# Cross-attention in fp32: Wo and V cross DRAM in fp32 and are split into parts on arrival; the row maximum moves to the end of its slot

## The chip, the cores and the metric

The kernel runs on one core of a Trainium2 chip. The core has five engines that run their own instruction queues and meet at semaphores: TensorE (PE, matrix products), VectorE (DVE), ScalarE (ACT), GpSimd (POOL) and SyncE (SP), which here issues nearly all DMAs. The metric is the time of one execution on the device, in microseconds.

## The reference

```python
a = layer_norm(ctx, gamma, beta)                  # ctx: 8 x 64 x 1024
Q = (x @ Wq.T)                                    # x: 8 x 1024 x 1024, 16 heads of 64
K, V = a @ Wk.T, a @ Wv.T
scores = Q K^T / 8  per head;  masked keys -> -inf
attn = softmax(scores over the 64 keys)
out = x + tanh(gate) * ((attn @ V) @ Wo.T)
```

Everything is fp32 and the output is 8192 x 1024.

## The kernel before

**Products in three parts.** Each fp32 operand is split into a high part, its rounding to fp32r, and a low part, the rest. `three` (lines 1192 to 1196) multiplies low x high, high x low and high x high. ScalarE makes the high parts by a rounding copy, VectorE (or GpSimd) the low parts by a subtraction.

**Stages.** First K, V and M are made: M holds Wq's product with K per batch, so that scores = x times M. PE works through 48 weight blocks in `TURNS`. M's blocks are copied from PSUM into the ring `m_stage` and stored to `m_scratch`, or straight into `b_raw`. V comes out in two column halves: ScalarE writes the scaled high part (`copy_v_hi`, line 718) and VectorE the low part (`split_v_lo`, 967), both into `v_out`; SyncE stores each half (`store_v`, 424).

**The main loop** has 224 steps in 32 rounds of 7. Rounds 0 to 15 make the scores of 512 rows each, rounds 16 to 31 the output. A round is one Strassen level: seven products P1, P5, P6, P3, P7, P2, P4, each a step of two groups of 12 matmuls (`item`, 1274). A step's left operand lies in `a_ring`: ScalarE writes its high part (`split_a_hi`, 738), VectorE the low part (`split_a_lo`, 974), one step ahead. The right operands of all seven products lie in `parts`, 16 KiB per partition each. In the score rounds they are refilled every 14 steps from M (`split_b_hi`, `split_b_lo`, `sum_b`; the steps are in `REFILL`). VectorE adds each product into `c_out` (`add_out`, 1058), and later products of the same round wait for these adds (1291 to 1302). An engine's order inside a step is written out in its loop: for VectorE lines 1136 to 1175. A step has two slots, z = 2s and 2s + 1.

**Softmax.** From step 98 on, units of 128 columns of scores run through slots fixed by `SOFT`: SyncE loads a unit (`load_s`, 455), which for a later unit waits until the one seven before it has been transposed; VectorE takes the row maximum (`row_max`), ScalarE the exponentials, VectorE the sums, GpSimd scales. The first 16 units are transposed by PE (`transpose_p`), rounded by ScalarE (`split_p_hi`) and their low part is made by VectorE (`split_p_lo`); PE transposes the next unit only when the last low part is there. Later units are turned by VectorE (`turn_blocks`), stored and fetched again by SyncE (`store_p`, `fetch_p`) and their low parts made by GpSimd. `values` (1265) multiplies by V, which lies in `v_diag` as two 64-wide diagonal blocks per head pair, in both parts, loaded per batch by `load_v` (489).

**Wo.** Wo's seven operands are three quarters of Wo and four sums of them. In steps 2 to 90 SyncE loads eighths of Wo (`load_wo_quarter`), VectorE makes the sums (`sum_wo`), ScalarE and VectorE split all seven pieces of each eighth (`round_wo`, `split_wo_lo`; 56 pieces, at the steps that `wo_step` gives) and ScalarE's queue stores them to `wo_split_scratch`. From step 106 on, SyncE loads both parts of the seven operands into `parts` in 28 DMAs (`load_wo_part`, 525; called at 608 to 610). Output rounds start with step 112.

Of the kernel before, what the change touches and what calls it, by code (L numbers as in the profile page):

```python
# [19 lines left out]
def xattn_kernel(nc, x, x_t, ctx_x, mask, wq_b, wk_t, wv_t, wo_t, gamma, beta, gate, out):  # L20
# [24 lines left out]
    v_scr = nc.dram_tensor("v_scratch", [B * S, NC, 2, P], F32, kind="Internal").ap()  # L45
    wo_scr = nc.dram_tensor("wo_split_scratch", [7, P, 2, HC, HD], F32, kind="Internal").ap()
# [3 lines left out]
    with ExitStack() as ctx:  # L50
# [35 lines left out]
        wo_sum = at("wo_sum", 208, [P, 4, QW])  # L86
        wo_ring = at("wo_ring", 212, [P, 3, 2, QW], F32R)
# [4 lines left out]
        v_out = [at("v_out0", 32, [P, CT, HC, 2, P], F32R), at("v_out1", 96, [P, CT, HC, 2, P], F32R)]  # L92
# [56 lines left out]
        wo_split_stored = sems("wo_split_stored", 3)  # L149
# [6 lines left out]
        v_hi_made = sem("v_hi_made")  # L156
        v_lo_made = sem("v_lo_made")
# [19 lines left out]
        v_in = sems("v_in", 2)  # L177
        s_in = sems("s_in", PROBS)
# [124 lines left out]
        WO_ORDER = (P1, P5, P7, P6, P3, P2, P4)  # L303
        WO_PIECES = 7 * 8

        def wo_step(w):
            return 14 * ((w + 6) // 9) + (0, 1, 3, 4, 4, 5, 6, 6, 7)[(w + 6) % 9]

        def wo_pieces(s):
            return [w for w in range(WO_PIECES) if wo_step(w) == s]  # L310

        def wo_quads(w):
            return [wo_quarter[:, w // 7 % 2, i, :] for i in range(4)]

        def wo_sums_by(w):

            return 4 * (w // 7) + (0, 1, 2, 3, 3, 3, 4)[w % 7]

        def wo_source(w):
            k = WO_ORDER[w % 7]  # L320
            if k in (P1, P3, P2):
                return wo_quads(w)[{P1: 0, P3: 3, P2: 2}[k]]
            return wo_sum[:, (P5, P7, P6, P4).index(k), :]
# [31 lines left out]
        def soft_slot(u):  # L355
            return SOFT[u]

# [24 lines left out]
        def _(sp):  # L382
# [4 lines left out]
            def load_wo_quarter(i):  # L387
# [3 lines left out]
                if i >= 2:  # L391
                    sp.wait_ge(wo_lo_made, 7 * (i - 1))
# [31 lines left out]
            def store_v(half):  # L424
                sp.wait_ge(v_lo_made, CT * (half + 1))
                to = v_scr[:, HC * half:HC * (half + 1)].rearrange("(i p) g t e -> p i (g t e)", p=P)
                sp.dma_start(to, v_out[half][:].rearrange("p i g t e -> p i (g t e)").bitcast(F32)
                             ).then_inc(v_stored[half], 16)
# [26 lines left out]
            def load_s(u):  # L455
                base, j = u // 8 * HT, u % 8
                if u == 0:
                    for i in range(3):
                        sp.wait_ge(wo_split_stored[i], 16 * ((WO_PIECES + 2 - i) // 3))
# [29 lines left out]
            def load_v(b, four):  # L489
                for h in range(2):  # L490
                    rr = slice(h * HEAD, (h + 1) * HEAD)
                    src = v_scr[b * S:(b + 1) * S, 4 * four:4 * four + 4, :, rr].rearrange("s g t e -> s (g t) e")
                    to = v_diag[rr, 4 * four:4 * four + 4, :, rr].rearrange("s g t e -> s (g t) e")
                    sp.dma_start(to.bitcast(F32), src).then_inc(v_in[four], 16)
# [30 lines left out]
            def load_wo_part(k, c):  # L525
                if c == 0:
                    sp.wait_ge(item_done, 2 * (14 * (B - 1) + 7 + k + 1))
                if k == 0 and c == 0:
                    for i in range(3):
# [155 lines left out]
        def _(act):  # L685
# [155 lines left out]
            for t in range(ITEMS):  # L841
# [10 lines left out]
                elif c == NC - 1 and half == 0:  # L852
                    for i in range(CT):
                        copy_v_hi(0, i)
# [511 lines left out]
```

## Time and profile before

| | us |
|---|---|
| median of 3 runs | 1492.25 (1492.04 to 1496.14) |
| the profiled execution | 1494.74 |
| its span, first to last instruction | 1493.0 |
| PE busy / VectorE / ScalarE / GpSimd | 1467.3 / 1163.7 / 894.1 / 537.7 |
| bytes read from and written to HBM | 198.26 MB, 145.75 MB |

The profile is of one execution. Times are us from the first instruction. Matmuls are pipelined: one of 512 columns is shown with about 390 ns, and the next starts some 0.23 us after it. "Idle" is the time for which an engine had nothing running before an instruction, put down to what ended it.

### The profile page before, as it was taken

The page shows a single profiled execution, that of the slowest core. Times are in us where ns is not written, and L with a number is a line of the kernel's source. Part 1 is how long each engine was busy: PE and PEld are TensorE (multiplying, and loading weights), DVE is VectorE, ACT ScalarE, POOL GpSimd, SP SyncE. Part 2 cuts the span into 40 slices and gives each one's busy share as a digit, 9 for nine tenths or more (in the row PEclk, how much of TensorE's full clock was granted, in tenths as well). Part 3 has the DMA queues.
Part 4 walks back from the last instruction along what each step waited for, and adds up shares of the span by engine and source line. Part 5 has one row for each costly group of instructions (what it writes and reads, how often), then busy time and mean ns, then how long its engine had stood idle before and what let it go on. Part 6 is the DMA issues. An engine that isn't in the chain of part 4 may idle for free.

```text
span 1493.0 us, 20136 instructions
## 1 busy us (share of the span) xinstructions
PE 1467.3 (98%) x6624; PEld 1194.6 (80%) x6624; DVE 1163.7 (78%) x1349; ACT 894.1 (60%) x1894; POOL 537.7 (36%) x364
## 2 busy tenths in 40 slices
PE   6999999999999999999999999999999999999999
PEld 5666788888888888888787788888888888888887
DVE  6445788787878787979866788888888888888843
ACT  4556655455555555555776667766777776677521
POOL 5334000000000000000124566677766667776640
PEclk9999999999999999999999999999999999999999
DMA  7699865657575747474579988788887878888732
GB/s 281 215 376 391 292 216 198 216 199 231 183 233 174 242 159 257 142 253 132 168 254 328 297 250 243 235 248 244 265 267 238 234 242 248 242 265 266 212 118 84
DMA packets 303144, 348.51 MB, mean 233 GB/s; under 512 B 35648, under 2 KB 177088, under 8 KB 303040
## 3 DMA queue, kind: packets, MB, share of 16 engines
q1 hardware_dynamic: 287808, 332.54, 70.2%
q10 hardware_dynamic: 15232, 14.68, 2.8%
q8 instruction: 53, 0.87, 0.2%
q14 instruction: 51, 0.42, 0.1%
HBM read 198.26 MB, written 145.75 MB: 230 GB/s over the span
## 4 chain that ended last, share of the span: by engine, by line
PE 89%; DVE 3%; DMA 3%; issue 1%; SPq 1%; ACT 1%; POOL 1%; DVEq 0%; ACTq 0%; POOLq 0%
PE banks L1194 29%; PE banks L1196 29%; PE banks L1195 29%; PE banks L1223 3%; DMA m_scratch<-m_stage 1%; DMA probs<-s_scratch 1%; DVE parts L983 1%; DMA b_raw<-m_stage 1%; DVE a_ring L977 1%; PE banks L1262 0%; SPq L475 0%; DVE b_raw L1003 0%; DMA b_raw<-m_scratch 0%; PE banks L1188 0%; DVE a_sum L1047 0%
## 5 line engine op out<-in xcount | busy, mean ns | idle before, releaser
L1194 PE MATMUL banks<-parts,a_ring 128*128 128x512 f32 x1792 | 699.5, 390 | 4.3 <-DVE a_ring L977 3.5
L1196 PE MATMUL banks<-parts,a_ring 128*128 128x512 f32 x1792 | 697.5, 389 | 0.0
L1195 PE MATMUL banks<-parts,a_ring 128*128 128x512 f32 x1792 | 697.2, 389 | 0.0
L1194 PEld LDWEIGHTS banks<-parts,a_ring 128*128 128x128 f32 x1792 | 336.4, 188 | 76.2 <-DVE a_ring L977 6.1
L1196 PEld LDWEIGHTS banks<-parts,a_ring 128*128 128x128 f32 x1792 | 336.3, 188 | 70.2
L1195 PEld LDWEIGHTS banks<-parts,a_ring 128*128 128x128 f32 x1792 | 336.4, 188 | 69.3
L977 DVE TENSOR_TENSOR a_ring<-a_sum,a_ring 128x1024 fp32r<-128x1024 f32 x128 | 227.1, 1774 | 76.6 <-ACT a_ring L748 76.5
L748 ACT CAST a_ring<-a_sum 128x1024 fp32r<-128x1024 f32 x128 | 134.3, 1049 | 233.8 <-PE banks L1196 205.3
L1072 DVE TENSOR_TENSOR c_out<-banks,c_out 128x1024 f32<-128x1024 f32 x158 | 192.0, 1215 | 100.4 <-PE banks L1196 98.6
L818 ACT ACTIVATE probs<-probs,neg_max 128x64 f32<-128x64 f32 x1024 | 258.6, 337 | 1.2 <-DVE neg_max L1086 1.2
L657 POOL TENSOR_TENSOR probs<-probs,row_rec 128x512 f32<-128x512 f32 x128 | 134.6, 1052 | 241.3 <-DVE row_rec L1095 241.3
L748 ACT CAST a_ring<-xq 128x1024 fp32r<-128x1024 f32 x96 | 100.8, 1050 | 168.9 <-PE banks L1196 162.4
L674 POOL MEMSET v_diag<- 128x2048 f32 x1 | 1.8, 1811 | 551.0 <-DVE parts L983 551.0
L663 POOL TENSOR_TENSOR p_parts<-p_by_key,p_parts 128x512 fp32r<-128x512 f32 x112 | 172.5, 1541 | 25.8 <-ACT p_parts L827 24.2
L977 DVE TENSOR_TENSOR a_ring<-xq,a_ring 128x1024 fp32r<-128x1024 f32 x96 | 118.0, 1229 | 35.3 <-ACT a_ring L748 35.3
L983 DVE TENSOR_TENSOR parts<-b_raw,parts 128x1024 fp32r<-128x1024 f32 x112 | 135.7, 1221 | 6.8 <-ACT parts L775 6.8
L839 ACT COPY xq<-banks 128x512 f32<-128x512 f32 x128 | 74.7, 584 | 81.2 <-PE banks L1196 75.7
L775 ACT CAST parts<-b_raw 128x1024 fp32r<-128x1024 f32 x112 | 114.3, 1048 | 2.7 <-DVE b_raw L1003 1.4
L1086 DVE TENSOR_REDUCE neg_max<-probs 128x8 f32<-128x512 f32 x128 | 85.0, 665 | 17.0 <-ACT probs L818 9.2
L634 POOL TENSOR_TENSOR w_ring<-w_raw,w_ring 128x512 fp32r<-128x512 f32 x48 | 64.8, 1372 | 77.6 <-ACT w_ring L690 77.6
L1003 DVE TENSOR_TENSOR b_raw<-b_raw 128x1024 f32<-128x1024 f32 x64 | 78.1, 1224 | 10.5 <-DMA b_raw<-m_stage 5.5
L964 DVE COPY m_stage<-banks 128x512 f32<-128x512 f32 x64 | 43.7, 690 | 53.6 <-PE banks L1223 47.1
(77 smaller groups left out, 1350.8 us busy)
## 6 DMA issues: line engine op xcount, KB each, us to landing
xq<-x_t SPq DMA_DIRECT2D x32, 1024.0 KB, 6.2
s_scratch<-c_out SPq DMA_DIRECT2D x64, 512.0 KB, 3.1
probs<-s_scratch SPq DMA_DIRECT2D x128, 256.0 KB, 4.2
c_out<-x SPq DMA_DIRECT2D x63, 512.0 KB, 5.5
out<-c_out SPq DMA_DIRECT2D x63, 512.0 KB, 4.2
b_raw<-m_scratch SPq DMA_DIRECT2D x29, 1024.0 KB, 6.8
m_scratch<-m_stage SPq DMA_DIRECT2D x16, 1792.0 KB, 14.0
p_scratch<-p_turned SPq DMA_DIRECT2D x448, 64.0 KB, 2.6
```

The costliest lines, as they stand in the source:

```text
L657: nc.gpsimd.tensor_tensor(pr, pr, rec, ALU.mult).then_inc(probs_done, 1)
L663: nc.gpsimd.tensor_tensor(p_parts[:, u % 2, 1, :], by_key(u), p_parts[:, u % 2, 0, :].bitcast(F32), ALU.subtract).then_inc(p_lo_made, 1)
L748: nc.scalar.copy(a_ring[:, s % 2, 0], a_source(n, k)).then_inc(a_hi_made, 1)
L775: nc.scalar.copy(parts[:, k, 0, c:c + 2, :], b_raw[:, B_HOME[k], c:c + 2, :]).then_inc(b_hi_made, 1)
L818: last = nc.scalar.activation(prob(u)[:, cols], prob(u)[:, cols], ACT.Exp, bias=neg_max[:, u % 2, g:g + 1])
L977: nc.vector.tensor_tensor(a_ring[:, s % 2, 1], a_source(n, k), a_ring[:, s % 2, 0].bitcast(F32), ALU.subtract).then_inc(a_lo_made, 1)
L983: nc.vector.tensor_tensor(parts[:, k, 1, c:c + 2, :], b_raw[:, B_HOME[k], c:c + 2, :], parts[:, k, 0, c:c + 2, :].bitcast(F32), ALU.subtra ...
L1072: nc.vector.tensor_tensor(c_out[:, q], bank_pair(n, k), to_add, ALU.add).then_inc(added, 1)
L1086: nc.vector.tensor_reduce(neg_max[:, u % 2, :], prob(u).rearrange("p (g s) -> p g s", s=S), AX.X, ALU.max, negate=True).then_inc(max_done, 1)
L1194: pe.matmul(to, wl, mh, start=first, stop=False, skip_group_check=joined)
L1195: pe.matmul(to, wh, ml, start=False, stop=False, skip_group_check=joined)
L1196: return pe.matmul(to, wh, mh, start=False, stop=last, skip_group_check=joined)
```

## The change

Wo: SyncE still loads the eighths, and VectorE makes the four sums, now at four steps in a row from 7 + 11i for eighth i; ScalarE's queue stores them unsplit (8 stores). Nothing is split before step 109. SyncE loads each operand whole in fp32, the three quarters from Wo itself and the four sums from the scratch, into the place of its low part. In steps 109, 110, 111, 113, 114, 115 and 116 ScalarE writes the high part in two halves, one per slot, and VectorE subtracts in place.

V: ScalarE alone writes V out, in fp32. The store and the loads carry one part. Each load lands in the place of the low part in `v_diag`; ScalarE and VectorE split it (two instructions each, on 64 partitions) three slots before its first product.

VectorE's order in a slot was sum, maximum, low part of probabilities, turn. It is now sum, low part, turn, maximum, V's low part, Wo's low part.

```diff
-    v_scr = nc.dram_tensor("v_scratch", [B * S, NC, 2, P], F32, kind="Internal").ap()
-    wo_scr = nc.dram_tensor("wo_split_scratch", [7, P, 2, HC, HD], F32, kind="Internal").ap()
+    v_scr = nc.dram_tensor("v_scratch", [B * S, D], F32, kind="Internal").ap()
+    wo_scr = nc.dram_tensor("wo_sum_scratch", [4, P, HC, HD], F32, kind="Internal").ap()
...
+        v_raw = at("v_raw", 120, [P, NC, 2, P])
+        wo_raw = [at(f"wo_raw{k}", 16 * k + 8, [P, HC, HD]) for k in range(7)]
...
+        LAST = 14 * (B - 1) + 7
+        WO_LOAD = {LAST + k + (1 if k < P2 else 2): k for k in range(7)}
+        WO_SPLIT = {LAST + k + (4 if k < P3 else 5): k for k in range(7)}
+        def wo_sum_step(i):
+            return 7 + 11 * i
...
+        def v_split(z):
+            return [(b, four) for b in range(B) for four in range(2) if values_at(16 * b + 4 * four) // 4 - 3 == z]
...
+            def load_wo_part(k):
+                sp.wait_ge(item_done, 2 * (LAST + k + 1))
...
+                sp.dma_start(wo_raw[k][:], src).then_inc(wo_part_in[k], 16)
...
-            def copy_v_hi(half, i):
+            def copy_v(half, i):
...
+            def split_wo_hi(k, h):
+                act.wait_ge(wo_part_in[k], 16)
+                part = slice(2 * h, 2 * h + 2)
+                nc.scalar.copy(parts[:, k, 0, part, :], wo_raw[k][:, part, :]).then_inc(wo_hi_made, 1)
...
+            def split_v_hi(b, four):
+                act.wait_ge(v_in[four], 32 * (b + 1))
+                for h in range(2):
+                    rr = slice(h * HEAD, (h + 1) * HEAD)
+                    nc.scalar.copy(v_diag[rr, 4 * four:4 * four + 4, 0, rr], v_raw[rr, 4 * four:4 * four + 4, 1, rr]
+                                   ).then_inc(v_hi_made, 1)
...
                     for u in units(soft_slot, z - EXP):
                         exponential(u)
+                    for b, four in v_split(z):
+                        split_v_hi(b, four)
+                    if s in WO_SPLIT:
+                        split_wo_hi(WO_SPLIT[s], z % 2)
...
+                for i in range(WO_QUARTERS):
+                    if 0 <= s - wo_sum_step(i) < 4:
+                        sum_wo(i, s - wo_sum_step(i))
                 for z in (2 * s, 2 * s + 1):
                     for u in units(soft_slot, z - SUM):
                         sum_rows(u)
-                    for u in units(soft_slot, z - MAX):
-                        row_max(u)
                     for u in units(split_slot, z):
                         if u < ON_PE:
                             split_p_lo(u)
                     for u in units(soft_slot, z - TURN):
                         if u >= ON_PE:
                             turn_blocks(u)
+                    for u in units(soft_slot, z - MAX):
+                        row_max(u)
+                    for b, four in v_split(z):
+                        split_v_lo(b, four)
+                    if s in WO_SPLIT:
+                        split_wo_lo(WO_SPLIT[s], z % 2)
...
-                        pe.wait_ge(wo_part_in[k], 64)
+                        pe.wait_ge(wo_lo_made, 2 * k + 2)
```

`split_v_lo` and `split_wo_lo` are the same with a subtraction. The waits for `v_lo_made` in the first stage become waits for `v_made`, and `values` waits for the new `v_lo_made` at the first unit of each load.

## Rows read from the trace of the kernel before

**Rows 1.** The page: busy us and share of each engine; the chain's shares.

```profile
PE 1467.3 (98%) x6624; PEld 1194.6 (80%) x6624; DVE 1163.7 (78%) x1349; ACT 894.1 (60%) x1894; POOL 537.7 (36%) x364
...
PE banks L1194 29%; PE banks L1196 29%; PE banks L1195 29%; PE banks L1223 3%; DMA m_scratch<-m_stage 1%; DMA probs<-s_scratch 1%; DVE parts L983 1%; DMA b_raw<-m_stage 1%; DVE a_ring L977 1%; PE banks L1262 0%; SPq L475 0%; DVE b_raw L1003 0%; DMA b_raw<-m_scratch 0%; PE banks L1188 0%; DVE a_sum L1047 0%
```

**Rows 2.** Busy times by stretch: its length, each engine (instructions), clock, DMA share, GB/s.

```profile
165.00:200.00 35.00, 33.84 (x145) 27.09 (x146) 33.13 (x32) 20.44 (x23) 0.00 (x0) 1.00 0.70 244
200.00:700.00 500.00, 500.00 (x2207) 414.01 (x2206) 414.10 (x418) 263.65 (x306) 0.00 (x0) 1.00 0.59 199
...
769.94:827.03 57.09, 53.87 (x253) 44.09 (x251) 39.80 (x60) 39.07 (x114) 21.87 (x15) 1.00 0.94 301
...
860.00:1480.00 620.00, 620.00 (x2737) 513.35 (x2737) 507.87 (x610) 408.13 (x1115) 413.45 (x266) 1.00 0.78 232
```

The five busy times are those of PE, its weight loads, VectorE, ScalarE and GpSimd.

**Rows 3.** Waits of PE: waited for, us in total, times, longest.

```profile
PE banks L1262 <- DVE p_parts L1108: 3.9, 3, 1.8
PE banks L1194 <- DVE a_ring L977: 3.5, 3, 1.4
...
PE banks L1194 <- POOL p_parts L663: 1.1, 1, 1.1
```

**Rows 4.** Timeline of VectorE and PE at the hand-over: start, us, what, idle before.

```profile
161.89 2.36 DVE L1003 TENSOR_TENSOR b_raw<-b_raw 128x1024 f32<-128x1024 f32 x2 [5.53 <-DMA b_raw<-m_stage]
164.16 1.22 DVE L977 TENSOR_TENSOR a_ring<-xq,a_ring 128x1024 fp32r<-128x1024 f32 x1
...
168.71 1.40 DVE L969 SCALAR_TENSOR_TENSOR v_out<-banks,v_scale,v_out 128x512 fp32r<-128x512 f32 x2
...
165.44 0.50 PE L1194 MATMUL banks<-parts,a_ring 128*128 128x512 f32 x1 [1.37 <-DVE a_ring L977]
```

**Rows 5.** DMA by stretch: its length, clock, share, GB/s.

```profile
134.00:161.00 27.00, 1.00 1.04 404
```

**Rows 6.** DMA issues: count, KB each, median us to landing.

```profile
parts<-wo_split_scratch SPq DMA_DIRECT2D x28, 512.0 KB, 7.7
...
v_scratch<-v_out SPq DMA_DIRECT2D x2, 2048.0 KB, 11.9
```

**Rows 7.** Groups by line: count, busy us, mean ns of one, idle before.

```profile
L983 DVE TENSOR_TENSOR parts<-b_raw,parts 128x1024 fp32r<-128x1024 f32 x112 | 135.7, 1221 | 6.8 <-ACT parts L775 6.8
...
L775 ACT CAST parts<-b_raw 128x1024 fp32r<-128x1024 f32 x112 | 114.3, 1048 | 2.7 <-DVE b_raw L1003 1.4 <-DMA b_raw<-m_scratch 0.8 <-issue 0.4
...
L1025 DVE TENSOR_TENSOR wo_ring<-wo_sum,wo_ring 128x256 fp32r<-128x256 f32 x32 | 13.0, 418 | 0.0
L782 ACT CAST wo_ring<-wo_sum 128x256 fp32r<-128x256 f32 x32 | 12.5, 403 | 2.6 <-DVE wo_sum L1021 1.5 <-issue 1.1
```

**Rows 8.** Timeline at step 55: VectorE's add, and PE's first product of P4.

```profile
464.78 1.22 DVE L1072 TENSOR_TENSOR c_out<-banks,c_out 128x1024 f32<-128x1024 f32 x1
...
466.37 0.39 PE L1194 MATMUL banks<-parts,a_ring 128*128 128x512 f32 x1
```

**Rows 9.** Timeline at the softmax start: late row maxima, and PE's waits for low parts.

```profile
800.12 0.69 DVE L1086 TENSOR_REDUCE neg_max<-probs 128x8 f32<-128x512 f32 x1 [2.38 <-DMA probs<-s_scratch]
...
805.21 0.63 PE L1262 MATMUL banks<-ident,probs 128*128 128x128 f32 x4 [1.41 <-DVE p_parts L1108]
...
817.62 0.69 DVE L1086 TENSOR_REDUCE neg_max<-probs 128x8 f32<-128x512 f32 x1 [1.94 <-DMA probs<-s_scratch]
...
819.05 0.63 PE L1262 MATMUL banks<-ident,probs 128*128 128x128 f32 x4 [1.81 <-DVE p_parts L1108]
```

**Rows 10.** Timeline at step 120: a GpSimd sum and VectorE's low part beside it.

```profile
852.07 2.38 POOL L651 TENSOR_TENSOR a_sum<-xq,a_sum 128x1024 f32<-128x1024 f32 x1
...
852.25 3.28 DVE L977 TENSOR_TENSOR a_ring<-a_sum,a_ring 128x1024 fp32r<-128x1024 f32 x1
```

**Rows 11.** Timeline of SyncE's queue: issues before the first store of turned probabilities.

```profile
814.07 2.96 SPq L531 DMA_DIRECT2D parts<-wo_split_scratch  x3
817.07 1.69 SPq L475 DMA_DIRECT2D p_scratch<-p_turned  x1
```

More of the change, by code:

```diff
@@ L298, in refills, with wo_quads @@
             return [(rnd, q) for rnd in range(B) for q in range(14) if refill_step(rnd, q) == s]
[L303 to L323, printed above, removed]
+        WO_QUAD = {P1: 0, P3: 3, P2: 2}
+        WO_SUMS = (P5, P7, P6, P4)
+        WO_QUARTERS = 2 * HC
+        LAST = 14 * (B - 1) + 7
[3 more added lines that the diff above has]
+            return 7 + 11 * i
+        def wo_quads(i):
+            return [wo_quarter[:, i % 2, quad, :] for quad in range(4)]
         def quad_rows(ap, n, q):
@@ L457, in load_s @@
                 if u == 0:
-                    for i in range(3):
-                        sp.wait_ge(wo_split_stored[i], 16 * ((WO_PIECES + 2 - i) // 3))
+                    for i in range(2):
+                        sp.wait_ge(wo_sum_stored[i], 16 * (WO_QUARTERS // 2))
                 elif u >= PROBS + ON_PE:
@@ L523, in after_product @@
                     store_quad(n, 2)
[L525 to L529, printed above, removed]
-                        sp.wait_ge(wo_split_stored[i], 16 * ((WO_PIECES + 2 - i) // 3))
-                sp.dma_start(parts[:, k, :, c, :].bitcast(F32), wo_scr[k, :, :, c, :]).then_inc(wo_part_in[k], 16)
+            def load_wo_part(k):
+                sp.wait_ge(item_done, 2 * (LAST + k + 1))
+                if k in WO_QUAD:
+                    r, c = divmod(WO_QUAD[k], 2)
+                    src = wo_t[r * HD:(r + 1) * HD, c * HD:(c + 1) * HD].rearrange("(c p) n -> p c n", p=P)
+                else:
+                    for i in range(2):
+                        sp.wait_ge(wo_sum_stored[i], 16 * (WO_QUARTERS // 2))
+                    src = wo_scr[WO_SUMS.index(k)]
+                sp.dma_start(wo_raw[k][:], src).then_inc(wo_part_in[k], 16)
             def slot(z):
@@ L548, in slot @@
                         load_x(y + 1)
-                    for i in range(8):
-                        if s == (2 + i if i < 2 else wo_step(7 * (i - 1) - 1) + 1):
+                    for i in range(WO_QUARTERS):
+                        if s == (2 + i if i < 2 else wo_sum_step(i - 2) + 5):
                             load_wo_quarter(i)
@@ L607, in _ @@
                 slot(z)
-                for i in range(28):
-                    if 2 * (14 * (B - 1) + 8) + (18 * i // 28) == z:
-                        load_wo_part(i // 4, i % 4)
+                if z % 2 == 0 and z // 2 in WO_LOAD:
+                    load_wo_part(WO_LOAD[z // 2])
             for g in range(2):
@@ L862, in _ @@
             for i in range(CT):
[L863 removed]
+                copy_v(1, i)
             for s in range(STEPS):
@@ L866, in _ @@
                     split_a_hi(s + 1)
-                for w in wo_pieces(s - 1):
-                    store_wo_split(w)
+                for i in range(WO_QUARTERS):
+                    if s == wo_sum_step(i) + 5:
+                        store_wo_sums(i)
                 if s > 0:
@@ L1104, in turn_blocks, with split_v_lo @@
                                     prob(u).rearrange("p (t h k) -> p h t k", h=4, t=4)).then_inc(turned, 1)
+            def split_v_lo(b, four):
+                dve.wait_ge(v_hi_made, 4 * b + 2 * four + 2)
+                for h in range(2):
+                    rr = slice(h * HEAD, (h + 1) * HEAD)
+                    hi, lo = (v_diag[rr, 4 * four:4 * four + 4, t, rr] for t in range(2))
+                    nc.vector.tensor_tensor(lo, v_raw[rr, 4 * four:4 * four + 4, 1, rr], hi.bitcast(F32), ALU.subtract
+                                            ).then_inc(v_lo_made, 1)
             def split_p_lo(u):
@@ L1121, in _ @@
                     split_k_lo(half)
-                elif c == NC - 1 and half == 0:
-                    for i in range(CT):
-                        split_v_lo(0, i)
             for q in range(2, 4):
@@ L1133, in _ @@
             sum_a(0, P5)
-            for i in range(2):
-                split_v_lo(1, i)
             for s in range(STEPS):
@@ L1141, in _ @@
                     split_a_lo(s + 1)
-                if s == 0:
-                    for i in range(2, CT):
-                        split_v_lo(1, i)
                 if n < ROUNDS:
```

97 lines of the change are left out of this document (38 added, 59 removed).

## The prediction

> **What bounds the kernel now.** I read the busy shares and the chain's shares first [rows 1]. TensorE (PE) is busy for 98% of the span, and its three product lines make 87% of the chain that ended last. VectorE is busy for 78% and ScalarE for 60%, so trimming either is worth only what PE waits for. Next I read PE by stretches [rows 2]. From 200 to 700 us and from 860 to 1480 us PE is busy for every microsecond, at 500.00 / 2207 = 0.2266 us a product, so a step of 24 products takes 5.44 us. The granted clock is 1.00 in every stretch, the 2.4 GHz level. In these 1120 us an edit can only lose time, unless it removes products, and this one removes none. PE idles 1.16 us in 165 to 200 and 57.09 - 53.87 = 3.2 us in 769.94 to 827.03. The waits of PE [rows 3] name who ends them: 3.9 us in three waits for VectorE's low part of the probabilities, 3.5 us in three waits for a_ring's low part, 1.1 us for GpSimd's low part. These 8.5 us, and some restart behind each, are nearly all that the change can give back. So three places count: the hand-over to the main loop, the start of the softmax with the new Wo work in it, and VectorE's slack in the dense stretches.
>
> **V out in fp32, and half of its store.** The four low halves of V's first column half fall where PE is dense: nothing. Those of the second stand in front of the first main steps. VectorE starts at 161.89 on b_raw, is busy from then on, and ends a_ring's first low part at 164.16 + 1.22 = 165.38; PE starts at 165.44 and has idled 1.37 [rows 4]. Two V instructions (1.40) lie before the second a_ring low part, two more behind it. Without them that part waits for ScalarE's high part instead (1.05, nearest row L775 [rows 7]), which needs the a_sum that VectorE makes just before: step 1 gains only about 0.1, but steps 2 to 5, which run off the same backlog, are freed: about 1.0 with restarts. What starts the backlog is the DMA of b_raw out of m_stage. The DMA engines are full from 134 to 161 us (share 1.04, 404 GB/s) [rows 5], and the first V store, of 2048 KB [rows 6], is issued in that stretch. It becomes 1024 KB: 1.05 MB / 404 GB/s = 2.6 us of a full queue. If all of it reaches b_raw, VectorE starts at 159.3, the first wait (1.37 and a restart of 0.1) goes, and PE's last V tile, which ends 1.37 before 165.44, is late next. Bounds: -3.1 (all that PE loses there) to -1.1 (queue unmoved). I take -2.8, since the queue is full right across.
>
> **The Wo sums in steps 7 to 88.** Removed: 56 high parts (ScalarE, 0.40), 56 low parts (VectorE, 0.42), 56 stores. Kept: the 32 sums, of the low parts' shape, at 0.42 [rows 7]. PE is dense there, so the removal is worth nothing. But the sums move, to four steps in a row from 7 + 11i. For i = 0 and 4 they fall on steps 7 to 10 and 51 to 54, where VectorE refills the seven B operands almost without a pause, and where the old order has next to no Wo work. There the add that P4 waits for ends at 464.78 + 1.22 = 466.00 and P4 starts at 466.37 [rows 8]: 0.37 of slack. Three sums at 0.42 (less when back to back) put about 1.0 ahead of it; I let pauses eat 0.2. So 0.8 - 0.37 + 0.1 = 0.5, twice, and i = 5 (two sums there) just about none: +1.0. Bounds: 0 (the sums fill pauses) to +1.5.
>
> **V split in the loop.** 16 loads are split by 32 ScalarE and 32 VectorE instructions of 256 elements; nearest rows 0.40 and 0.42 [rows 7], bounds 0.25 to 0.6 each. Each split is 0.8 on each engine, last in its slot, three slots before its products. The first stands ahead of a low part of the probabilities on which PE already waits; the row maximum now goes behind that part (0.6 saved), so +0.2 net. Of the 15 others those in the dense stretch meet VectorE at 507.87 / 620 = 82% [rows 2]: hidden, 0. Were their cover gone, the seven that end an odd slot would cost some 0.3 each, +2.
>
> **Wo's operands split between steps 109 and 116.** Added in 57 us: 14 high parts at 1.05 (ScalarE, nearest row L775) and 14 low parts at 1.22 (VectorE, L983) [rows 7]. Busy times were 39.07 and 39.80 of 57.09 [rows 2]. Now they are 39.07 + 14.7 = 53.8 and 39.80 + 17.1 = 56.9: both are full, VectorE wholly. The 28 part loads of 512 KB become 7 of 1024 KB (14.7 MB to 7.3 MB) [rows 6], where the DMA share was 0.94 [rows 2]; they lead their use by three steps and are on no path. What was on the path is in [rows 9]. VectorE idled 2.38 and 1.94 us for a row maximum whose scores were late, and only then did the low part for which PE waited (1.41 at 805, 1.81 at 819). The new order puts that part in front of the maximum. That removes the second wait and, with quicker scores, the first: -3.5 with restarts. Against it stand the halves. I followed both engines from step 109, each serving its queue in order. ScalarE falls about 1 us behind per step, so that the high part of unit 13 ends near 808 in place of 804; the low part before PE's transposes of unit 14 comes 1.3 us late, that before unit 15 some 2.1, an earlier one 0.3: 3.8 with restarts. In addition VectorE and GpSimd block each other. A GpSimd sum from 852.07 to 854.45 makes a_ring's low part, begun at 852.25, last 3.28: it ends 1.08 after the sum does [rows 10], where it takes 1.22 alone [rows 4]. GpSimd is busy 21.87 of 57.09 [rows 2], mostly just behind a VectorE instruction of one input; I count one of its long sums on the path, at about half of 2.38: +1.2. So 3.8 + 1.2 - 3.5 = +1.5. Bounds: -3.5 (all hidden) to +7 (VectorE's 56.9, five or six halves blocked for 1 us, and some 2 us in which it must idle for ScalarE). The Trainium skill has the exclusion as a rule (SBUF — State Buffer, Who interferes with whom): a VectorE instruction with two SBUF inputs and a GpSimd instruction that reads SBUF never run together, and whichever starts first blocks the other. By that rule the trace agrees, at 3.28; and all 14 new low parts are of that sort, which speaks for the dear end of the range.
>
> **Steps 117 to 122.** PE waits for GpSimd's part near 845 (1.1) [rows 3] and for the a_ring part of [rows 10] (1.4). Their chain comes from SyncE, which stores the first turned probabilities late: it issues three Wo part loads in 2.96 us just before [rows 11]. Without those it fetches them some 2.7 us earlier, and ScalarE, which heads its queue with that wait, follows. I take half of 2.5 + restarts: -1.4; bounds -2.9 to +1 (the last halves of step 116 in front of it).
>
> **Sum.** -2.8 + 1.0 + 0.2 + 1.5 - 1.4 = -1.5. The profiled execution took 1494.74 (span 1493.0 and 1.74 around it), 2.49 above the median shown. It would take 1493.2, and the median 1490.7.
>
> **Rivals.** (a) The softmax start clears: the halves fit into pauses, of which each engine has 17 to 18 us. All three places give back: -3.1 + 0.5 + 0.2 - 3.5 - 2.9 = -8.8, 1483.5. For it: those pauses and the lighter DMA. Against: 56.9 of 57.1 us. (b) Slower: the halves fill VectorE from step 109 to 118, and a_ring's low parts come behind them. A step of 24 + 3 products takes at least 6.1 us there, and the two a_ring parts 2.3 of them, so they lead PE by some 4 us; it decides once the backlog passes that. Price +7 there, nothing back in 117 to 122, V's odd splits +1: -2.8 + 1.0 + 0.2 + 7 + 1 = +6.4, 1498.7. For it: the ledger and [rows 10]. Against: steps 112 and 117 have no halves and let it catch up. (c) The change does what it says and the relief doesn't reach PE: the V store isn't what b_raw waits for, and the waits at 805 and 819 are only replaced: -1.1 + 1.0 + 0.2 + 0.3 = +0.4, 1492.7.
>
> **How the numbers follow.** Forecast 0.40, (a) 0.27, (b) 0.22, (c) 0.11. What can be told from no change is 0.3%, 4.5 us: faster is below 1487.8, slower above 1496.7. The forecast's own range is 1487 to 1494. Faster: (a) and a tail of the forecast, 0.30; slower: (b), 0.22; same 0.48. Range 1484.5 to 1497.5: it leaves out the far halves of (a) and (b).
>
> **What would show it.** Step 0 starts at or just after 164.0 us: the V store's part is right; at 165.4 it is not. PE waits of about 0.4 for an add at P4 in steps 13 and 55: the sums. From step 109 to 116, VectorE above 95% busy and PE waits for its p_parts that add up to 4 to 5 us: the halves. None of these waits, and (a) holds; waits for a_ring too, and (b) does. A first fetch of turned probabilities before 826 us: SyncE's relief. I am wrong if PE has gaps in 860 to 1480, or if its gaps between 165 and 860 add up to under 4 or over 16 us.

## The result and the profile after

The changed kernel takes 1517.39 us (median of 4 runs, 1517.17 to 1519.59). The kernel before took 1493.65 beside it (4 runs, 1492.04 to 1496.14). The ratio is 1.0161, with a 95% interval of 1.0141 to 1.018: 24 us slower, where 1.5 faster was forecast. The profiled execution took 1517.17, its span 1515.4.

The page after, shares of busy time, then those waits of PE that lie in the main loop (waited for, us in total, times, longest); they answer to [rows 1] and [rows 3]:

```profile
PE 1476.1 (97%) x6624; PEld 1200.3 (79%) x6624; DVE 1176.2 (78%) x1331; ACT 901.1 (59%) x1884; POOL 537.4 (35%) x364
...
PE banks L1195 <- DVE a_ring L976: 15.3, 9, 2.1
...
PE banks L1263 <- DVE p_parts L1115: 7.0, 3, 3.0
...
PE banks L1195 <- DVE c_out L1071: 0.7, 2, 0.4
```

The busy shares hardly moved. What moved are the waits: a_ring's low part from 3.5 us in three waits to 15.3 in nine, the low part of the probabilities from 3.9 to 7.0. GpSimd's 1.1 has gone. (These are idle times as the profile has them, counted from the modelled end of the last product. In the text behind, a gap or a wait of PE is counted from when the next product was due, 0.227 us behind the start of the last one, which gives 0.16 more: the gaps of 2.24 below are the 2.08 of the profile.) The same stretches as in [rows 2], and the length of one half-clock episode (length, busy time of PE, PEld, DVE, ACT, POOL with instructions, granted clock, DMA share, GB/s):

```profile
165.00:200.00 35.00, 35.00 (x156) 29.00 (x155) 29.95 (x27) 20.10 (x22) 0.00 (x0) 1.00 0.68 233
200.00:700.00 500.00, 499.26 (x2201) 412.48 (x2200) 394.54 (x364) 244.59 (x251) 0.00 (x0) 1.00 0.52 176
769.94:827.03 57.09, 51.74 (x224) 41.93 (x223) 52.89 (x64) 45.20 (x113) 23.84 (x14) 0.91 0.56 183
...
860.00:1480.00 620.00, 606.95 (x2656) 500.38 (x2657) 514.10 (x631) 416.86 (x1145) 411.90 (x267) 0.99 0.77 229
...
1040.70:1044.10 3.40, 3.40 (x10) 2.67 (x9) 3.40 (x4) 1.29 (x6) 3.25 (x2) 0.51 0.32 77
```

The first stretch is now dense. The last, full before, has lost 13 us of PE and some clock. The sharpest reading comes from the start of each step's first product on PE, after minus before, in us: -3.4 at step 7; -1.7 at step 70; -0.7 from 104 to 112; +3.5 at 113; +6.5 at 119; +4.9 at 120; +5.0 from 121 to 134; then +7.2 at 135 and up at each of 149, 163, 177, 191 and 205; +22.4 at 206 and to the end. So about 17.5 of the 22.4 us come from six places 14 steps apart.

This is the first of them, between 940 and 950 us: VectorE, ScalarE and GpSimd in turn (start, us, engine, line, form; idle before and what ended it).

```profile
940.89 0.65 DVE L1085 TENSOR_REDUCE neg_max<-probs 128x8 f32<-128x512 f32 x1
943.72 3.82 DVE L1110 TENSOR_TENSOR v_diag<-v_raw,v_diag 64x256 fp32r<-64x256 f32 x2 [2.19 <-ACT v_diag L829]
947.58 1.23 DVE L1071 TENSOR_TENSOR c_out<-banks,c_out 128x1024 f32<-128x1024 f32 x1
948.72 1.22 DVE L976 TENSOR_TENSOR a_ring<-a_sum,a_ring 128x1024 fp32r<-128x1024 f32 x1
...
940.95 2.02 ACT L814 ACTIVATE probs<-probs,neg_max 128x64 f32<-128x64 f32 x8
942.87 0.82 ACT L829 CAST v_diag<-v_raw 64x256 fp32r<-64x256 f32 x2
...
943.42 2.40 POOL L649 TENSOR_TENSOR a_sum<-xq,a_sum 128x1024 f32<-128x1024 f32 x1
945.78 1.48 POOL L661 TENSOR_TENSOR p_parts<-p_by_key,p_parts 128x512 fp32r<-128x512 f32 x1
```

Read it in this order. VectorE is free at 941.5, and its next instruction is V's low half. That needs ScalarE's high half, which is queued behind eight exponentials and ends at 943.69: 2.19 of idling. In that pause GpSimd started a sum, at 943.42, which holds VectorE's first low half up to its end at 945.82 (2.38 in place of 0.42); GpSimd's next instruction then holds the second (1.41). The two halves take 3.82 in place of 0.84. The add and a_ring's low part, for which PE waits, were queued behind. Step 135 starts at 949.99, 2.24 late. The add starts 6.0 us after step 134 does (941.62). Before, at the same place, it started 0.2 us after it (936.65), and a_ring's low part, itself slowed by a GpSimd sum, ended at 941.93, 0.84 ahead of step 135 (942.77):

```profile
936.85 1.23 DVE L1072 TENSOR_TENSOR c_out<-banks,c_out 128x1024 f32<-128x1024 f32 x1 [0.27 <-PE banks L1196]
938.97 2.96 DVE L977 TENSOR_TENSOR a_ring<-a_sum,a_ring 128x1024 fp32r<-128x1024 f32 x1 [0.89 <-ACT a_ring L748]
```

So a block by GpSimd and some idling lay in this stretch before as well: 1.74 of block on a_ring's part (2.96 - 1.22) and 1.16 of idling (0.27 + 0.89). The 2.19 and the 3.82 took the place of these and brought about 3.1 us more; 0.84 of it went into the margin and 2.24 reached PE.

Behind two of the six gaps the products then come every 0.43 us in place of 0.227 for 3.4 us. PE after the gap before step 191:

```profile
1309.25 0.50 PE L1195 MATMUL banks<-parts,a_ring 128*128 128x512 f32 x1 [2.08 <-DVE a_ring L976]
...
1309.83 0.39 PE L1197 MATMUL banks<-parts,a_ring 128*128 128x512 f32 x1
1310.05 0.45 PE L1195 MATMUL banks<-parts,a_ring 128*128 128x512 f32 x1
1310.30 0.63 PE L1196 MATMUL banks<-parts,a_ring 128*128 128x512 f32 x1
1310.73 0.63 PE L1197 MATMUL banks<-parts,a_ring 128*128 128x512 f32 x1
```

The granted clock is 0.51 over such an episode (the last row of stretches), the 1.2 GHz level; each costs half its length, 1.7 us. Six gaps of 2.24 are 13.4, two episodes 3.4, and restarts (the second product behind such a gap starts 0.34 us after the first in place of 0.227) make the rest of 17.5. Between steps 112 and 118 lie two more, of 3.4 us behind a wait of 2.55 (791.1 to 793.7) and of 6.8 us, 815.3 to 822.1, around the end of one of 3.12 (813.1 to 816.2).

The new groups of instructions by line (busy, mean ns, idle before and its releaser):

```profile
L1110 DVE TENSOR_TENSOR v_diag<-v_raw,v_diag 64x256 fp32r<-64x256 f32 x32 | 33.4, 1043 | 21.3 <-ACT v_diag L829 20.8
L1024 DVE TENSOR_TENSOR parts<-wo_raw,parts 128x1024 fp32r<-128x1024 f32 x14 | 18.3, 1304 | 0.9 <-ACT parts L784 0.9
L784 ACT CAST parts<-wo_raw 128x1024 fp32r<-128x1024 f32 x14 | 14.6, 1045 | 0.0
L829 ACT CAST v_diag<-v_raw 64x256 fp32r<-64x256 f32 x32 | 12.8, 399 | 0.4
```

ScalarE's halves last what the nearest rows said (0.40 and 1.05). VectorE's V halves have a median of 0.42 but a mean of 1.04, and in front of them it idles for ScalarE for 20.8 us. That line alone holds the reason.

### The profile page after: what moved, and what is told of

The parts are those of the page before. It is cut to its first block, busy times and chain, and to the rows that moved or that the text cites. A ratio compares the mean times of both kernels' runs of the same rounds, so it can differ in the third digit from the quotient of the medians.

```text
span 1515.4 us, 19964 instructions
## 1 busy us (share of the span) xinstructions
PE 1476.1 (97%) x6624; PEld 1200.3 (79%) x6624; DVE 1176.2 (78%) x1331; ACT 901.1 (59%) x1884; POOL 537.4 (35%) x364
## 4 chain that ended last, share of the span: by engine, by line
PE 84%; DVE 7%; ACT 3%; issue 3%; DMA 1%; SPq 1%; POOL 0%; DVEq 0%; ACTq 0%
PE banks L1195 27%; PE banks L1196 27%; PE banks L1197 27%; PE banks L1224 3%; DVE a_ring L976 2%; ACT probs L814 2%; DVE c_out L1071 1%; DVE parts L982 1%; DMA m_scratch<-m_stage 1%; DVE b_raw L1002 1%; ACT xq L842 0%; PE banks L1263 0%; ACT v_diag L829 0%; DVE row_sum L1090 0%; PE banks L1189 0%
## 5 line engine op out<-in xcount | busy, mean ns | idle before, releaser
L1195 PE MATMUL banks<-parts,a_ring 128*128 128x512 f32 x1792 | 702.8, 392 | 16.0 <-DVE a_ring L976 15.3
L976 DVE TENSOR_TENSOR a_ring<-a_sum,a_ring 128x1024 fp32r<-128x1024 f32 x128 | 215.8, 1686 | 81.0 <-ACT a_ring L746 81.0
L661 POOL TENSOR_TENSOR p_parts<-p_by_key,p_parts 128x512 fp32r<-128x512 f32 x112 | 169.3, 1512 | 26.6 <-ACT p_parts L823 25.7
L1090 DVE TENSOR_REDUCE row_sum<-probs 128x8 f32<-128x512 f32 x128 | 85.5, 668 | 0.0
```

The source lines that it names most:

```text
L661: nc.gpsimd.tensor_tensor(p_parts[:, u % 2, 1, :], by_key(u), p_parts[:, u % 2, 0, :].bitcast(F32), ALU.subtract).then_inc(p_lo_made, 1)
L976: nc.vector.tensor_tensor(a_ring[:, s % 2, 1], a_source(n, k), a_ring[:, s % 2, 0].bitcast(F32), ALU.subtract).then_inc(a_lo_made, 1)
L1090: nc.vector.reduce_sum(row_sum[:, u % 2, :], prob(u).rearrange("p (g s) -> p g s", s=S), AX.X).then_inc(sum_done, 1)
L1195: pe.matmul(to, wl, mh, start=first, stop=False, skip_group_check=joined)
```

## The experiments

"Step n" below is the start of its first product against that of the kernel before (runs' profiles). A profile's start of the main loop differs from another's by itself: in the six kernels with the old way of V, step 7 lies between -1.0 and +0.9, mean -0.05. Times are medians; the kernel before took 1493.5 to 1494.3 beside them.

**e1 and e2: place, or time?** e1 moves the V splits that ended an odd slot one slot on:

```diff
- ... if values_at(16 * b + 4 * four) // 4 - 3 == z]
+ ... if (values_at(16 * b + 4 * four) // 4 - 2) // 2 * 2 == z]
```

> The changed kernel with one edit: the V splits that sit at the end of an odd slot (7 of them in the dense stretch) move to the even slot behind it, so that VectorE makes a_ring's low part first. Theory (place): each of the 2.24 us gaps of PE in steps 121 to 205 comes from V's low halves standing before the add and a_ring's low part while they wait for ScalarE and then for GpSimd's sum. Then no gap over 0.3 us is left after 865 us and the clock stays at 1.00 there: 17.5 us less than 1517.4, about 1500. Rival (amount): VectorE lacks the time for 0.8 us more wherever it is put: gaps go to other steps, 1512 to 1518.

e2 moves ScalarE's high halves alone, one slot ahead of VectorE's low halves:

```diff
-                    for b, four in v_split(z):
+                    for b, four in v_split(z + 1):
                         split_v_hi(b, four)
```

> The changed kernel with ScalarE's high half of each V split one slot earlier; VectorE's low halves stay where they are. It tells the wait for ScalarE from the block by GpSimd. If only the wait for ScalarE (behind 2 us of exponentials) costs: the gaps go, 1500. If only GpSimd's sum blocks: they stay at 2.24 us, 1517. Theory (both in turn): VectorE starts the halves some 2 us earlier, ahead of the sum, may be blocked once by a shorter GpSimd instruction: gaps under 1 us, 1501 to 1507.

e1: 1504.06, ratio 1.0072 [1.0056, 1.0089]. The gaps of 2.24 are gone, and 0.50 at each following step, with some new waits around step 121, came in their place: 4 us more than expected, so the place was most of the loss, not all. e2: 1500.64, ratio 1.0049 [1.0034, 1.0064], and from 861 us on PE has no gap at all: the difference stays at +5.7. Its stretch of the dense part, and the V splits' two groups:

```profile
860.00:1480.00 620.00, 618.72 (x2730) 512.32 (x2731) 521.55 (x637) 420.03 (x1149) 420.73 (x269) 1.00 0.78 230
```

```profile
L1110 DVE TENSOR_TENSOR v_diag<-v_raw,v_diag 64x256 fp32r<-64x256 f32 x32 | 26.1, 817 | 0.6
L829 ACT CAST v_diag<-v_raw 64x256 fp32r<-64x256 f32 x32 | 12.9, 404 | 0.4
```

The idle before the low half fell from 21.3 to 0.6 us with the same instructions in the same number. VectorE's work was never the trouble; it is even still blocked now and then (mean 0.82). What cost was VectorE standing for ScalarE, with everything else queued behind. Of the three readings put down for e2 this fits the one that I did not hold, that the wait for ScalarE alone costs; e12 below shows the share that the block had as long as VectorE waited.

**e3 and e4: one part alone.** e3 is the kernel before with the V part only, e4 the changed kernel with V as before.

> The kernel before with only the V part of the change. Theory: it carries the gain at the hand-over (-3.4 us at step 12) and the loss in the dense stretch (+17.5), and about +1.5 at the first low part of the probabilities: 1493.7 + 15.6 = 1509. Rival (the parts need each other: the gaps come only with the later row maximum): the hand-over alone, 1490 to 1492.

> The changed kernel with V as before (Wo part and row maximum kept). Theory: no gap after 865 us, the hand-over gain is lost: 1517.4 - 17.5 + 3.4 - 1 = 1502. Rival (Wo's part is what costs in the dense stretch too): above 1508.

e3: 1511.64, ratio 1.0122 [1.0107, 1.0137], 2.6 above what was expected. Step 7 at -3.2, step 134 at -1.7, then the six gaps (and three half-clock episodes): +17.4 at the end. e4: 1500.19, ratio 1.0047 [1.0032, 1.0062]. The gaps of 0.5 at steps 13 and 55, step 70 at +1.1, step 112 at +0.5, step 118 at +7.2, +5.3 at the end, nothing after 861 us. The parts add up: +17.4 and +5.3 against +22.4.

**e5: the row maximum last, alone.**

```diff
                     for u in units(soft_slot, z - TURN):
                         if u >= ON_PE:
                             turn_blocks(u)
+                    for u in units(soft_slot, z - MAX):
+                        row_max(u)
```

> The kernel before with the row maximum moved to the end of its slot, V and Wo as before. My blind working gave this edit the whole of the two waits at 805 and 819 us (-3.5). Theory 'the maximum was in the way': both waits go, steps 112 to 118 come out 2.5 to 3.5 us earlier, total about 1490.5 to 1491.5. Rival 'the order moves the wait': the low part goes first, but the maximum, and with it the exponentials and the later units, come as late as before; the waits change place, and the total stays within 1 us of 1494.

1492.48, ratio 0.9989 [0.998, 0.9998]. In its trace the wait at 819 is gone, that at 805 went from 1.57 to 0.81, that at 732 from 0.80 to 0.19; one of 0.90 for GpSimd's part at 831 is new. At the end -1.9 in the profile, -1.0 by the medians. In between the two theories: at most half of what I had given this edit.

**e6 and e7: Wo.** Both are the kernel before with the Wo part alone. e6 moves the sums off the refill steps; e7 leaves them and makes ScalarE's Wo halves a slot early.

```diff
-            return 7 + 11 * i
+            return 14 + 14 * (i // 2) + 4 * (i % 2)
```

```diff
-                    if s in WO_SPLIT:
-                        split_wo_hi(WO_SPLIT[s], z % 2)
+                    if (z + 1) // 2 in WO_SPLIT:
+                        split_wo_hi(WO_SPLIT[(z + 1) // 2], (z + 1) % 2)
```

> The kernel before with the Wo part alone (V and the order of the row maximum as before), and its sums moved from steps 7 + 11 i to steps 14 + 14 (i / 2) + 4 (i mod 2), which keeps them off steps 8 to 13 of every 14, where VectorE refills the B operands. Theory 'the sums stood in front of P4's add and a_ring's low part': no gap of 0.5 at steps 13 and 55 and none of 0.17 at 69, difference to the kernel before 0.0 from step 7 to 101. Rival 'the gaps come from something else of the Wo part' (its loads, its stores): they stay, or show at other steps, +1.2 in all. Steps 109 to 120 have the halves as in the changed kernel: if these alone are the cost there, +6.5 to +7.5 by step 118 and +5.5 at the end, total 1499 to 1500; if half of it came from V, +3, total 1496.5.

> The kernel before with the Wo part alone, and ScalarE's high halves of Wo one slot earlier, so that VectorE's low half finds its high half made. Theory 'as with V, VectorE stands waiting for ScalarE, whose half is queued behind the exponentials': the loss of steps 112 to 118 falls from about +7 to +2 or +3, total about 1496. Rival 'both engines have more work than time there and GpSimd's sums block VectorE': the order of the halves frees nothing, the loss stays at +6 or more, total 1500 or above.

e6: 1501.09, ratio 1.0045 [1.0031, 1.0058]. No gap from step 7 to 101: the difference is +0.85 throughout. So the sums stood in the way, as forecast. By step 118 it is +8.6, 1 more than expected. e7: 1503.45, ratio 1.0057 [1.0041, 1.0074], step 118 at +10.3, a loss of 8.7 from step 109 on against e6's 7.8: the mend that healed V made this worse. Here VectorE doesn't wait for ScalarE (0.9 us of idle in the changed kernel's row above). What it does instead, VectorE, then GpSimd, in the changed kernel from 784 us:

```profile
784.73 1.21 DVE L1024 TENSOR_TENSOR parts<-wo_raw,parts 128x1024 fp32r<-128x1024 f32 x1
785.86 3.42 DVE L976 TENSOR_TENSOR a_ring<-xq,a_ring 128x1024 fp32r<-128x1024 f32 x1
789.21 1.21 DVE L1071 TENSOR_TENSOR c_out<-banks,c_out 128x1024 f32<-128x1024 f32 x1
790.34 0.67 DVE L1085 TENSOR_REDUCE neg_max<-probs 128x8 f32<-128x512 f32 x1
790.94 1.21 DVE L1024 TENSOR_TENSOR parts<-wo_raw,parts 128x1024 fp32r<-128x1024 f32 x1
792.07 0.67 DVE L1090 TENSOR_REDUCE row_sum<-probs 128x8 f32<-128x512 f32 x1
792.77 0.20 DVE L1094 RECIPROCAL row_rec<-row_sum 128x8 f32<-128x8 f32 x1
792.89 0.64 DVE L1115 TENSOR_TENSOR p_parts<-banks,p_parts 128x512 fp32r<-128x512 f32 x1
...
784.75 3.46 POOL L649 TENSOR_TENSOR a_sum<-xq 128x1024 f32<-128x1024 f32 x1
```

VectorE has no pause from one end to the other. The Wo half (784.73) and GpSimd's sum (784.75) start together; the sum first waits out the half and lasts 3.46 in place of 2.4, then a_ring's part waits out the sum and lasts 3.42 in place of 1.22. The low part of the probabilities (792.89) is last in this queue, and PE's next transposes, at 793.68, wait 2.55 us for it. VectorE's instructions of 770 to 834 us took 7.0 us in all above the medians of their forms, against 0.6 before.

**e8, e9 and e10: V without the stall.** On the kernel before: e8 has the V part with high halves a slot early, and the first batch's two halves a slot earlier still. e9 adds the row maximum last. e10 is e9 with the first batch's halves one slot later than in the changed kernel, behind the first low part of the probabilities, and the high halves early as in e2:

```diff
- ... if values_at(16 * b + 4 * four) // 4 - 3 == z]
+ ... if values_at(16 * b + 4 * four) // 4 - 3 + (b == 0) == z]
```

> The kernel before with the V part alone, ScalarE's high halves of V one slot before VectorE's low halves, and both halves of the first batch one slot earlier still. Theory: the hand-over gain stays (-3.25 at step 7), no gap at 135, 149, 163, 177, 191 and 205 (0 in place of 2.24 each and their half clock), and the first split costs 0 to 1 us at steps 102 to 104: -2.2 to -3.2 at the end, total 1491 to 1492 against 1494, a gain of 0.15 to 0.2%. Rival 'a split costs wherever it stands, since VectorE has no slack': 0.5 or more at each of the 14 later splits, total above 1498.

> The kernel of e8 (V part alone, its halves early) with the row maximum last in its slot as well; Wo as before. Theory 'the two gains are apart, V's at the hand-over (-2.9 at step 7) and the maximum's at 732, 805 and 819 us (-1.9)': -3.5 to -4.5 at the end, total 1489.5 to 1490.5 against 1493.5. Rival 'both reach the same row of waits around 805 to 860, and what one gives the other can't give again' (both came to -1.9 at the end): -2 to -3, total about 1491.5.

> As e9, but of V's first batch both halves go one slot after the place of the changed kernel, not one before: the low half then stands behind the low part of the first probabilities. In e3 that low half in front of it made PE wait 2.44 in place of 0.80 at 731, in e8 one slot earlier 1.11, with 0.47 at step 103 besides. Theory 'it is the order around unit 0': 0 to 0.3 there and none at step 103, so 0.5 to 1.0 less than e9, total 1489 to 1490. Rival: the low half is then late for its own products at step 104 (PE waits for v_lo_made, 0.5 to 2), and nothing is gained on e9.

e8: 1492.41, ratio 0.9991 [0.9982, 0.9999]. e9: 1490.87, 0.9978 [0.9969, 0.9987]. Both lie 0.4 above their forecasts. e10: 1488.91, 0.9968 [0.9955, 0.998], the best version, 4.8 us under the kernel before. Its waits of PE in the main loop (the rest of its list lies ahead of it):

```profile
PE banks L1203 <- DVE a_ring L984: 2.4, 2, 1.6
...
PE banks L1203 <- POOL p_parts L668: 0.7, 1, 0.7
PE banks L1271 <- DVE p_parts L1123: 0.3, 1, 0.3
```

The 8.5 us of [rows 3] are down to 3.4, both as the profile counts. Around step 104 the order decided: e3, with the low half in front of the first low part of the probabilities, waits 2.44 there; e8, a slot earlier, 1.11 with 0.47 at step 103; e10 nothing. From step 104 on e10 gains 2.6 where e5 gained 1.5 and e8 lost none; the extra is at step 118, where e5 and e8 wait 0.9 for GpSimd's part (831 us) and e10 does not; why it doesn't I have not taken apart.

**e11, e12 and e13: GpSimd's sums in two.** From step 90 on each sum for a_ring is two instructions of half the size: in e11 on the Wo part alone, in e12 on e3, in e13 on e10.

```diff
-                nc.gpsimd.tensor_tensor(a_sum[:, A_SUM[k]], *sum_operands(n, k)).then_inc(sum_made, 1)
+                one, two, op = sum_operands(n, k)
+                to, c = a_sum[:, A_SUM[k]], HC // 2
+                nc.gpsimd.tensor_tensor(to[:, 0:c], one[:, 0:c], two[:, 0:c], op)
+                nc.gpsimd.tensor_tensor(to[:, c:], one[:, c:], two[:, c:], op).then_inc(sum_made, 1)
```

> The kernel before with the Wo part alone, and each of GpSimd's sums for a_ring from step 90 on as two instructions of half the size, so that VectorE can start between them. In e6 a_ring's low parts lasted 3.4 instead of 1.22 four times between 784 and 830, each begun just after a sum; VectorE's instructions there took 6.4 in all above their medians. Theory 'the block by GpSimd's sums is a large part of the loss': blocked time falls to about half, the loss of steps 111 to 118 from +7.8 (e6: +0.87 to +8.64) to +3 to +5, total 1496 to 1498. Rival 'VectorE and ScalarE simply have more work than time there': +7 or more stays, total 1500 or above. The two waits of over 3 with half clock behind them should go if the first theory holds.

> The kernel of e3 (V part alone, halves in one slot as in the changed kernel), GpSimd's sums as two instructions of half the size. In e3 PE waited 2.24 at each of steps 135, 149, 163, 177, 191 and 205, where VectorE's first low half lasted 2.38 behind a sum that ScalarE's late half had let go first. Theory 'wait for ScalarE and block by GpSimd add up': the block falls by about 1.2, each gap from 2.24 to about 1.0, and the half clock goes with it: +6 in place of +19 over these steps, total about 1499 against 1511.6 for e3. Rival 'the wait for ScalarE alone sets it': the gaps stay above 2, total 1508 to 1512. Rival 2: VectorE is blocked by the second half too, and nothing changes.

> The kernel of e10 (V part with its halves re-placed, row maximum last, Wo as before) with GpSimd's sums as two instructions of half the size. In e11 that took the wait at step 121 from 1.4-1.6 to 0.48, in e12 to 0.63; e10 waits 1.76 there. Theory 'the wait at step 121 is the block by a GpSimd sum': it falls to about 0.6, total about 1488 against 1488.9 for e10 and 1493.7 for before. Rival: GpSimd's sums get longer by as much (blocked twice) and delay the units' normalising, so that new waits between 800 and 850 eat it: 1489 to 1490.

e12: 1503.75, ratio 1.0062 [1.0048, 1.0075], against 1511.64 for e3. Its gaps at 135, 149 and so on measure 1.41 to 1.43 in place of 2.24 (about 1.0 was expected), and no half clock follows any of them. VectorE and GpSimd at the first:

```profile
939.58 2.99 DVE L1120 TENSOR_TENSOR v_diag<-v_raw,v_diag 64x256 fp32r<-64x256 f32 x2 [3.03 <-ACT v_diag L840]
...
939.55 1.31 POOL L657 TENSOR_TENSOR a_sum<-xq,a_sum 128x512 f32<-128x512 f32 x1
940.82 1.47 POOL L658 TENSOR_TENSOR a_sum<-xq,a_sum 128x512 f32<-128x512 f32 x1
```

So wait and block add up: 0.83 of each gap went with half the length of the sum, and the second low half is still held (1.40). The half clock behind these gaps went with it. The whole is 4.8 above the forecast: besides the gaps, step 104 lies 3.2 later than in e3, half of it by a half-clock episode behind the wait at 732 (2.44 long in both kernels, without an episode in e3). e11: 1499.71, ratio 1.0038 [1.0024, 1.0052], 1.7 above the forecast. The loss of steps 109 to 118 is 5.2, against 7.8 in e6. The gaps up to step 118 add up to 7.1 in e11 and 7.0 in e6, so the difference is clock: e6 has an episode of 3.4 and one of 6.8 (1.7 + 2.9 lost), e11 one of 3.4. Five waits of at most 2.4 cost less than three of the same sum, two of them above 3. e13: 1489.09, ratio 0.9968 [0.9957, 0.998], the same as e10. The wait at step 121 fell from 1.76 to 0.66 as expected, but the one at 840 grew from 0.87 to 1.49 and one of 0.35 came up: the rival was right too.

**e14 and e15: what is left.** e14 is the changed kernel with all its parts and four mends (e6's place for the sums, ScalarE's V halves a slot early as in e2, the first batch's halves a slot later as in e10, GpSimd's sums in two). e15 is e11 with ScalarE's high halves cut to 64 of 512 columns, so that part of Wo's high parts isn't made.

> The changed kernel whole (V, Wo and row maximum), with four mends: ScalarE's V halves one slot before VectorE's, the first batch's both a slot later, Wo's sums moved off the refill steps, GpSimd's sums in halves. If the causes found so far are all: hand-over and steps 102 to 104 as in e10 (-3.1 at step 109), halves of Wo as in e11 (+2.5 from step 109 to 121 there; the order of the row maximum may give 0 to -1 of it), nothing after 861: -1.5 to 0 at the end, total 1492 to 1494 against 1517.4 for the changed kernel. Rival 'V's halves and Wo's meet around step 111 to 121 and cost more together': total 1496 or above.

> The kernel of e11 (Wo part alone, GpSimd's sums in halves) with ScalarE's high halves of Wo cut to 64 of each 512 columns; the other columns of the high parts aren't written, so this leaves work out. It takes some 0.8 of 1.05 off each of 14 ScalarE instructions, 11 us of 55, and changes nothing for VectorE and GpSimd. Theory 'VectorE is what is full': the loss of steps 109 to 118 stays near e11's +5.2 (within 1), total 1499 to 1500. Rival 'ScalarE's time for the halves is the cost': the loss falls to 2 or less, total 1496 or below.

e14: 1493.35, ratio 0.9995 [0.9986, 1.0003]: the kernel before again, 24 us under the changed one. In e15 (1498.73, ratio 1.0033 [1.0022, 1.0044]) the stretch 770.11 to 833.33 reads, with e11's below it:

```profile
770.11:833.33 63.22, 56.00 (x254) 45.33 (x253) 58.69 (x73) 41.79 (x128) 28.26 (x19) 0.97 0.59 186
```

```profile
770.11:833.33 63.22, 57.62 (x262) 46.58 (x261) 58.19 (x74) 52.16 (x129) 28.29 (x19) 0.97 0.58 184
```

ScalarE has 10.4 us less to do, VectorE as much as before, and the loss of steps 109 to 118 is 6.0, not less than e11's 5.2. ScalarE's time is off the path there. That VectorE is what is full fits its 58 of 63 us, but no run takes VectorE's Wo halves away, so this is argued and not shown.

## Why the prediction was wrong

**V out and the hand-over (-2.8): right.** Step 7 comes at -3.4. In the ten kernels with the new V it lies between -3.8 and -1.2, mean -2.8. VectorE starts on b_raw at 159.27, where my working had 159.3. Its wait for that DMA is 1.8 to 3.0 us in these ten kernels and 5.2 to 5.5 in the seven with the old V. From step 0 on PE has no gap, and V's last tile is what it does until 163.81.

```profile
159.27 2.36 DVE L1002 TENSOR_TENSOR b_raw<-b_raw 128x1024 f32<-128x1024 f32 x2 [3.02 <-DMA b_raw<-m_stage]
...
163.58 0.39 PE L1197 MATMUL banks<-w_ring,a_parts 128*128 128x512 f32 x1
163.81 0.39 PE L1195 MATMUL banks<-parts,a_ring 128*128 128x512 f32 x1
```

**The Wo sums (+1.0): right in mechanism.** The waits for the add at steps 13 and 55 are there (gaps of 0.52 and 0.53), and e6 takes them away by place alone. The whole is +1.6, with restarts and a gap at step 69 that I had put at none.

**V split in the loop (+0.2, the rest "hidden, 0"): here the prediction failed.** The failed step is "those in the dense stretch meet VectorE at 507.87 / 620 = 82%: hidden, 0", with its uncovered price of 0.3 each. Measured: 2.24 for each of six, and 1.7 for each half-clock episode behind them, 17.5 in all. The 0.3 counted VectorE's work alone. It left out that a low half is two waits in one: for ScalarE, whose half I had put behind the exponentials of the slot without asking when these end (2.2 us of a stopped VectorE), and for GpSimd, which starts a sum in that pause (3.0 us more over both halves, of which 1.7 had lain on a_ring's part before). The margin that took this was 0.84. The idle 18% was real, but it lay in other places; e2 and e10 show that the same work does fit. I had even written that a block by GpSimd costs about half of 2.38 in the Wo part, and hadn't asked it of V. The first split (+0.2) cost +1.0 at step 104; its order against the low part of the probabilities decides it (e10: none).

The Trainium skill states the exclusion (SBUF — State Buffer, Who interferes with whom): a VectorE instruction with two SBUF inputs and a GpSimd instruction that reads SBUF exclude each other for a whole instruction, and the order of issue, not the shape, decides who waits. The traces agree: 0.42 became 2.38 for a V half behind a sum, and 2.4 became 3.46 for a sum behind a Wo half.

**The Wo halves (+1.5, bounds -3.5 to +7): the mechanism right, the size wrong.** From step 109 to 119 it is +7.2, just above the dear bound. The gaps of 2.55, 3.12 and 0.57 there stand against 1.57 and 1.97 before: +2.7, where my working had +1.5. The other 4.5 are half clock (by the lengths of the episodes 1.7 for the first and some 3.0 for the second), a term that I did not have, since the clock of before was 1.00 in every stretch. Inside the waits two errors partly cancel: the row maximum gives -1.4 to step 118 (e5), not -3.5, and the halves alone add 3.5 of waits (e6: 7.0 against 3.5), not 3.8 + 1.2. VectorE was busy for 52.89 of 57.09 us (93%) in the stretch for which I had summed 56.9. e15 clears ScalarE's time. How the waits divide between VectorE's own queue and the block by GpSimd (7.0 us over the medians) stays open: e11 shortened the blocks (4.8 over the medians, against e6's 6.4), and the gaps' sum did not fall.

**Steps 117 to 122 (-1.4): the mechanism right, the size near.** Over all the steps named it is -0.9 (+5.9 at step 117, +5.0 at 122); the gain lies from 119 to 121, -1.6, and PE no longer waits for GpSimd's part. The first fetch of turned probabilities did not come before 826 us, as my sign asked, but at 831.79 (before: 827.52), at steps that come 5.9 later. That alone could be the delay's doing. But against its own step 117 the fetch lies 1.0 to 2.4 us ahead in all nine kernels with the Wo part, e14 among them, whose steps are only 1.4 late, and 0.5 to 2.0 behind in the eight without it. So SyncE's relief is real.

The text named the gaps in 860 to 1480 as what would make it wrong, and so they did. Rival (b) had the sign: its +7 for steps 109 to 118 is there, though by waits for the probabilities and by clock rather than for a_ring; its "V's odd splits +1" is the 17.5.

## What to carry to other kernels

A moved instruction is priced by what it waits for at its place, not by its length: an engine that works in order stops with all that is queued, and spare busy share elsewhere doesn't help. When two engines make the halves of one operand, look at the idle time in front of the second engine's half. Where it is large (V: 21.3 us), put the first engine's half a slot earlier; where there is none (Wo: 0.9), that gives nothing, and in e7 it cost. Put neither in front of an instruction for which PE already waits. In these kernels a gap of PE of 2.2 us or more could cost more than the gap.

## What the runs showed of the hardware

Before, PE held the 2.4 GHz level through every wait of the main loop, 1.97 us at most. With longer waits the granted clock fell to the 1.2 GHz level, for 3.4 us 18 times and for 6.8 us twice in the main loops of all the profiles. The fall came between 1.1 us before and 1.4 us after the end of a wait of PE. Behind each of the eight waits of 3.1 us or more it fell; with waits of 2.2 to 2.6 us it fell in some cases and not in others (in the changed kernel with two of six alike gaps of 2.24); with waits of 2.13 us or less it never did. In e12, with 1.41 at the same six places, PE kept 2.4 GHz at all of them. What decides between alike gaps these runs don't show.

VectorE and GpSimd blocked each other both ways: 0.42 became 2.38 and 1.22 became 3.42 on VectorE, 2.4 became 3.46 on GpSimd, and with the sum split in two VectorE's first V half lasted 1.56 in place of 2.38.
